# Issuing the row maxima's transfer from ScalarE's queue instead of SyncE's in a fused attention kernel

## The reference

```python
for c in range(NUM_NOD):                 # 6 nodes, each for 16 sequences
    q = ew[c, 0] * (nodes[in_q] @ We[eq] + be[eq])
    k = ew[c, 1] * (nodes[in_k] @ We[ek] + be[ek])
    v = ew[c, 2] * (nodes[in_v] @ We[ev] + be[ev])
    o = _mha(q, k, v, Wq[c], Wk[c], Wv[c], Wo[c])     # 8 heads of 16, softmax over 256 keys
    nodes[c] = act_w[c] * o + q
```

## Time and profile before

| what | value |
|---|---|
| median of 3 runs | 1064.5 us (1063.66 to 1065.46) |
| profiled execution | 1066.53 us, of which 1064.6 us are its span |
| PE / DVE / ACT / POOL busy | 92% / 79% / 68% / 42% of the span |
| TensorE's granted clock | 0.982 of full speed over the span |

### The profile page before, as it was taken

One profiled execution on the slowest core, in us unless ns is written; L12 is line 12 of the kernel. 1 busy time (PEld: TensorE's weight loads), 2 busy tenths in 40 slices (PEclk: granted clock), 3 DMA queues, 4 the chain that ended last, 5 costly groups with the idle time before them and its releaser, 6 DMA issues.

```text
span 1064.6 us, 26783 instructions
## 1 busy us (share of the span) xinstructions
PE 980.8 (92%) x9705; PEld 699.2 (66%) x9705; DVE 838.1 (79%) x1805; ACT 723.3 (68%) x1601; POOL 447.6 (42%) x874
## 2 busy tenths in 40 slices
PE   8989999998799999999999999999999999999995
PEld 4765656555566766767666777667666676676763
DVE  5466777766689997878888899888788888888896
ACT  3345666665577777777677778877777777777775
POOL 3522222233343344335444448843443344443365
PEclk9889999999899999999999999999999999999998
DMA  9100000006466666666676676576566666657641
GB/s 234 27 1 1 1 0 0 0 2 87 64 108 99 99 92 105 97 104 96 102 107 92 102 105 113 109 117 102 94 107 98 101 97 104 104 93 106 103 74 35
DMA packets 72407, 87.33 MB, mean 82 GB/s; under 512 B 11642, under 2 KB 45950, under 8 KB 72286
## 3 DMA queue, kind: packets, MB, share of 16 engines
q1 hardware_dynamic: 70686, 83.69, 48.8%
q0 software_dynamic: 800, 1.98, 0.8%
q10 hardware_dynamic: 800, 0.05, 0.0%
HBM read 6.90 MB, written 2.10 MB: 8 GB/s over the span
## 4 chain that ended last, share of the span: by engine, by line
PE 38%; DMA 20%; DVE 11%; ACT 9%; SPq 8%; POOL 6%; issue 6%; DVEq 0%; POOLq 0%; ACTq 0%
PE bank L1288 37%; DMA mst<-mrows 19%; SPq L503 8%; ACT region L816 4%; POOL hl L591 3%; POOL hl L588 3%; DVE region L1154 2%; DVE region L1086 1%; ACT qk L781 1%; ACT qk L780 1%; DVE region L970 1%; DVE region L1081 1%; ACT region L792 1%; PE bank L1624 1%; DVE region L1074 1%
## 5 line engine op out<-in xcount | busy, mean ns | idle before, releaser
L1154 DVE TENSOR_REDUCE region<-bank 128x2 f32<-128x512 f32 x768 | 489.3, 680 | 120.2 <-PE bank L1288 119.7
L816 ACT ACTIVATE region<-bank 128x512 f32<-128x512 f32 x768 | 406.5, 599 | 68.0 <-PE bank L1288 65.2
L1288 PE MATMUL bank<-st 48*128 48x256 f32 x3072 | 309.6, 326 | 5.3 <-DVE region L1154 4.5
L588 POOL TENSOR_TENSOR hl<-qk,one_col 128x512 fp32r<-128x512 f32 x96 | 100.1, 1043 | 395.0 <-ACT qk L781 395.0
L1288 PEld LDWEIGHTS bank<-st 48*128 48x128 f32 x3072 | 243.1, 189 | 19.7 <-DVE region L1154 5.3
L1288 PE MATMUL bank<-region 128*32 128x256 f32 (+3 forms) x3554 | 250.0, 377 | 2.7 <-DVE region L1181 1.0
L1288 PEld LDWEIGHTS bank<-region 128*32 128x32 f32 (+2 forms) x3554 | 130.7, 117 | 86.1 <-issue 17.0
L1288 PE MATMUL bank<-mst,ones 64*128 64x512 bf16 x768 | 150.1, 387 | 37.2 <-DMA mst<-mrows 34.3
L591 POOL TENSOR_TENSOR hl<-qk,hl 128x512 fp32r<-128x512 f32 x96 | 122.9, 1280 | 7.5
L838 ACT ACTIVATE mrows<-bank 24x256 bf16<-24x256 bf16 x96 | 35.8, 373 | 128.6 <-PE bank L1624 128.6
L1288 PEld LDWEIGHTS bank<-mst,ones 64*128 64x128 bf16 x768 | 37.0, 92 | 97.8 <-DMA mst<-mrows 51.9
(11 more groups left out here) (193 smaller groups left out, 1269.6 us busy)
## 6 DMA issues: line engine op xcount, KB each, us to landing
st<-hl SPq DMA_DIRECT2D x576, 128.0 KB, 4.3
out<-xall POOLq DMA_DIRECT2D x14, 128.0 KB, 3.7
mst<-mrows SPq DMA_DIRECT2D x96, 12.0 KB
xall<-in_L_attn_hidden_states SPq DMA_DIRECT2D x1, 768.0 KB, 7.0
cst<-in_constants SPq DMA_DIRECT2D x1, 514.5 KB, 3.9
xT<-in_L_ffn_Wq SPq DMA_DIRECT2D x1, 384.0 KB
xT<-in_L_ffn_Wk SPq DMA_DIRECT2D x1, 384.0 KB
xT<-in_L_ffn_Wv SPq DMA_DIRECT2D x1, 384.0 KB
```

The costliest lines, as they stand in the source:

```text
L588: pool.tensor_tensor(to[:, K_HI::Q_HI - K_HI, :], qk[a.n % 2], one_col[:, :].unsqueeze(2).to_broadcast([P, 2, T]), ALU.mult)\
L816: act.activation(to, x_bank(x, k, e)[:, :].rearrange("p (j q) -> p j q", j=2), ACT.Exp).then_inc(B["exp_ok"], 1)
L1154: dve.tensor_reduce(mx[s.n % 2][:, to:to + 2], s_bank(s, k, e)[:, :].rearrange("p (j k) -> p j k", j=2), AX_X, ALU.max, negate=True).then_ ...
L1288: return pe.matmul(o, w, x, start=start, stop=stop, skip_group_check=skip)
```

## The change

The function `maxima_rows` moves from SyncE's program to ScalarE's. It is called right behind `copy_rows`, with the same waits on the same semaphores, and the DMA is then issued by ScalarE's sequencer on ScalarE's own queue. SyncE is left with the stacks. The exponentials, copies and matmuls are the same, in the same order.

```diff
--- before.py
+++ after.py
@@ SyncE
-            def maxima_rows(m):
-
-                old = at_slot(m.n, 2)
-                if old is not None:
-                    sp.wait_ge(B["x_ps"], old.n * UNITS + UNITS)
-                else:
-                    sp.wait_ge(S["ones_ok"], 3)
-                sp.wait_ge(B["mt_ok"], m.n + 1)
-                sp.dma_start(mst[m.n % 2][0:(2 * MROW - 1) * MSTEP + 1:MSTEP, :, :], mrows[m.n % 2][:, :]).then_inc(m_in[m.n % 2], 16)
-
             def phase(t, a, s, m, x, d, z, w, v):
-                if m is not None:
-                    maxima_rows(m)
                 if a is not None:
                     stack(a)
@@ ScalarE
+            def maxima_rows(m):
+
+                old = at_slot(m.n, 2)
+                if old is not None:
+                    act.wait_ge(B["x_ps"], old.n * UNITS + UNITS)
+                else:
+                    act.wait_ge(S["ones_ok"], 3)
+                act.wait_ge(B["mt_ok"], m.n + 1)
+                act.dma_start(mst[m.n % 2][0:(2 * MROW - 1) * MSTEP + 1:MSTEP, :, :], mrows[m.n % 2][:, :]).then_inc(m_in[m.n % 2], 16)
+
...
                 if m is not None:
                     copy_rows(m)
+                    maxima_rows(m)
                 if x is not None:
                     exps(x, 1)
```

## The result

The changed kernel takes 1094.75 us in the median of 4 runs (1093.14 to 1095.94), the kernel before 1064.08 us in 4 runs beside it (1063.26 to 1065.46). The ratio is 1.0286, with a 95% interval of 1.0265 to 1.0306: 30.7 us slower. The forecast was 1082 us, with a range from 1062 to 1104.

The account below looks back on a forecast made before the run. Bound: a two-phase loop through the stack, its last wait named `mst`, 8.14 us a phase. (0.69 - 0.42 + 0.10) / 2 = 0.185 us a phase, times 93 = 17.2 us, gave 1082 us, range 1062 to 1104.

Parts of the forecast that it names:

- The loop over two phases: TensorE, copies of q and k, split, stack, `mst` landing: 16.16 us per two phases, so changes count half per phase, times 93.
- its own case: The forecast's central outcome, 1072 to 1092 us, given a chance of 0.52.
- The issue on ScalarE, 0.77 us, and the delay of 0.69: One DMA issue ahead of ScalarE's exponentials takes 0.77 us (lower bound 0.44) and starts them 0.69 us later.
- What that delay costs: 0.69 / 2 x 93 = 32 us: Copies of q and k, and the stack behind them, come 0.69 us later; half counts per phase, over 93 phases.
- this loop at 8.03 us: One-phase loop through q and k copies, GpSimd's split, maxima's split and rows' copy: 8.03 us, just below the stack's.
- The phase of pure work: TensorE's phase without waits grows from 7.60 to about 7.87 us, as unit 3's matmuls stall 0.2 to 0.3 us.
- the gain of 0.42: Wait for `mst` removed by issuing at once on ScalarE; the two-phase loop shortens by at most 0.42 us, until the stack binds.
- 0.1 us of interference with the stack (4.7 us): The 12 KB now travel while the stack is in flight, making it land 0.1 us later; bounds nothing and 0.5.
- The shared issue: Rival: ScalarE's issue waits for SyncE's, 0.3 to 0.6 us more; 1096 to 1128 us, chance 0.23.
- The short issue: Rival: ScalarE's issue takes only 0.44 us, so the trade turns; 1048 to 1067 us, chance 0.22.
- The whole win: Rival: the stack is not the next bound, phase is 7.87 us of work; 1039 us, chance 0.03.
- The signs that I named: Right: `mst` waits under 10 us, stack waits 20 to 50. Wrong: staying `mst` waits, or maxima's split ending waits.

Follow-up runs that it names:

- `act_twin`: Kernel before, `mst` still sent by SyncE, plus a second transfer of the same rows issued by ScalarE into a dead tile; 1106.98 us against 1062.93, ratio 1.0409.
- the fillers: Two kernels: the kernel before with two, then three, extra unread copies on ScalarE behind the rows' copy; 1076.87 us (ratio 1.0119) and 1106.32 us (1.0405).
- `act_filler2`: Kernel before, transfer still on SyncE, with three extra unread copies on ScalarE behind the copy of the rows; 1106.32 us against 1062.93, ratio 1.0405.
- `sp_hold1`: Kernel before, all on SyncE, with `mst` issued after five of the stack's DMAs and ahead of the sixth; 1050.86 us against 1063.83, ratio 0.9864.

## Why the prediction was right, and which terms were off

The side and the range held: slower, by 31 us and not 17. The loop over two phases and the size of the issue were right. Two terms of the sum were off by about 6 to 12 us each, both to the slow side, and a third, of 4.7 us, was not there. The time lies outside the 1072 to 1092 us that the forecast called its own case, so it was the width of the range that held it.

- **The loop over two phases and its half.** Right for a small delay: 0.26 us cost 13 us (forecast by half, 12). For 0.78 us it was 43 and not 36, which the third point takes up.
- **The issue on ScalarE, 0.77 us, and the delay of 0.69.** Right: 0.741 us (740/741/1369). The first exponential started 598.54 - 594.20 = 4.34 us into the phase, where it was 573.05 - 569.41 = 3.64, 0.70 later. The copies of q and k ended at 601.33, 7.13 us into the phase and not 6.43.
- **What that delay costs: 0.69 / 2 x 93 = 32 us.** Mis-sized. `act_twin` has this delay and no gain and costs 44, of which a part is its second transfer; from the fillers it is about 38. What the sum left out stands in the waits that rose: the split of the maxima, from 5.3 to 13.9 us in the twin, 15.6 and 16.4 in `act_filler2` and the kernel after. The text had this loop at 8.03 us, "just below the stack's", and priced it at nothing. The 8.03 was right: its parts take 3.66 + 3.61 + 0.75 = 8.02 us in the kernel after. They are the way from the end of the rows' copy to the end of the copies of q and k, from there to the end of the split (both in the median), and from there to the end of the next rows' copy (the shortest). The price of nothing was not. A bound on one phase costs nothing only if no phase would have been shorter, and before the change 4 in 10 phases of the steady part were shorter than 8.05 us, the shortest 7.61. That this and the next point are the whole of the 6 to 12 us is argued from the waits and these lengths, not shown.
- **The phase of pure work.** Mis-sized: forecast 7.87 us, measured 8.06 (594.20 to 602.26, without a wait at its end). The eight matmuls of unit 3 now run as four and four. They ran in 0.83 us; now they take from 591.49 (0.59 long) to 592.76 (592.26 + 0.50), 1.27 us, so 0.44 more and not 0.2 to 0.3. The exponentials' wait itself is 0.18 at the matmuls; the rest is that the second four no longer overlap the first. The forecast called this phase "hidden while the loop is longer than that". It is not hidden: no phase in the middle of the kernel after is shorter than 8.05 us, and a quarter of them last no more than 8.06.
- **"ScalarE can issue [...] in every phase and not only where SyncE was free", the gain of 0.42.** This is the step that failed in its mechanism. It issues earlier than SyncE did, 3.61 instead of 4.55 us into the burst, but the last of the stack's six had as a rule already gone out at 3.2 (585.72 to 588.9). The 4.1 us from issue to use that I took from a fast phase were 4.94 in the phase above. The transfer waited behind the stack, wherever it was issued from. It gained only in the 34 of 91 phases where one of SyncE's issues ran long (over 1.0 us in nearly all of them, 0.7 and 0.9 in two). The forecast's 19.5 us became 7 to 13.
- **0.1 us of interference with the stack (4.7 us).** Not there: the stack landed at 8.43 and 8.37, as before at 8.43.

The forecast's sum was 32.1 - 19.5 + 4.7 = 17.3 us. In its place stands 44 - 13 = 31 by the twin, or 38 - 7 = 31 by the fillers. Both give the measured 30.7 by construction, since the gain was found as the difference; they are no check.

**The rivals.** The shared issue came nearest in its time (1096), nearer than the forecast, and is not what happened: on ScalarE it would show as an issue row above 0.77, and the row reads 740/741, with 1369 the longest. SyncE's own issues did not grow either (597 ns in the median before and after). The short issue needed 0.44 us. The whole win, 1039, needed an earlier landing of `mst` and of the stack. `sp_hold1` shows how far the first of these goes by itself: 1051. **The signs that I named:** the `mst` waits were to fall under 10 us and stayed at 13.7 and 22.9, and those for the stack were to be 20 to 50 and were 4.1. Both follow from the step that failed: `mst` was still the last to land in most phases. The first exponential started 0.88 us after the copy of the rows ended (597.66 to 598.54), as I had said, 0.85 to 0.9. A chain in which the split of the maxima ends waits was named as a sign against me, and it came in part.

## What to carry to other kernels

When a small transfer lands together with a large one, look at what was issued ahead of it before moving it to another queue. Here the order of issue over all queues decided for the most part, and another engine's queue brought nothing that one DMA held back on the same queue did not bring better. An issue on a compute engine is an instruction like any other, 0.74 us here, and belongs to every loop that runs through that engine. A second bound that lies 0.1 to 0.3 us (of 8) below the mean phase isn't free. Compare it with the shortest phases and not with the mean: those that would have been shorter can no longer make up for the long ones.

## What the runs showed of the hardware

- Of DMAs issued from SyncE, ScalarE or GpSimd within one burst, the small one landed by its place in the order of issue: behind all six of 128 KB 8.3 to 8.7 us after the first issue, behind five 7.65 to 8.08, behind four 6.55 (SyncE) or 7.10 (ScalarE). Holding the last one back by one place cost the stack nothing (8.40 against 8.43), by two 0.6 us.
- The issue of the same transfer took 0.741 us on ScalarE, 0.767 on SyncE and 0.585 on GpSimd in the median. The 12 KB transfer cost more to issue than one of 128 KB (0.597); the four small loads at the start cost 0.47 each.
- Of the 576 issues of the stack in the kernel after, 47 took 1.06 to 2.02 us instead of 0.6. Every one of them coincided with a 16 KB packet of the queue that fetches instructions, and so did 42 of the 515 that took under 0.7 us. Such a packet alone does not make an issue long, then, and that the one causes the other wasn't tried.
- ScalarE's copies overlap: two in a row (0.51 and 0.29 us) put off the end of the work behind them by only 0.26 us. Of their time, 0.18 us was idle before; and they start 0.41 us apart.
